# A four-stage graph network on one core: head sums in PSUM, eight edge-term slots, word rows made four sets ahead, and dense stages in two-bank instructions

## The reference

```python
# block 0, four layers, then a layer norm and two linear layers with layer norms
agg = jax.ops.segment_sum(x[src], dst, num_segments=N)
h = (1.0 + eps[i]) * x + agg
h = jax.nn.relu(_bn(h @ W1[i] + b1[i], bn1_g[i], bn1_b[i]))
h = _bn(h @ W2[i] + b2[i], bn2_g[i], bn2_b[i])
if i < L - 1:
    h = jax.nn.relu(h)
h = _bn(h, obn_g[i], obn_b[i])
...
x = h + x_in
# block 1: x @ W_S, plus a segment sum of x[col] @ W_T and edge terms
# block 2, four layers
msg = jax.nn.relu(x[src] + ea)
h = x + jax.ops.segment_sum(msg, dst, num_segments=n)
h = jax.nn.silu(h @ W1[l] + b1[l]) @ W2[l] + b2[l]
# block 3, attention with 8 heads of 16
score = K[src] * Q[dst] / jnp.sqrt(jnp.float32(dh)) * Eh
score = jnp.exp(jnp.clip(score.sum(-1, keepdims=True), -5.0, 5.0))
wV = jax.ops.segment_sum(V[src] * score, dst, num_segments=N)
Z = jax.ops.segment_sum(score, dst, num_segments=N)
h_attn = (wV / (Z + ATTN_EPS)).reshape(N, D)
```

## Time and profile before

| | us |
|---|---|
| runs | 10679.4, 10709.26, 10701.52 |
| median | 10701.52 |
| profiled execution | 10682.69 |
| span of its trace | 10681.0 |

### The profile page before, as it was taken

One profiled execution on the slowest core, in us unless ns is written; L12 is line 12 of the kernel. 1 busy time (PEld: TensorE's weight loads), 2 busy tenths in 40 slices (PEclk: granted clock), 3 DMA queues, 4 the chain that ended last, 5 costly groups with the idle time before them and its releaser, 6 DMA issues.

```text
span 10681.0 us, 246329 instructions
## 1 busy us (share of the span) xinstructions
PE 7847.9 (73%) x65479; PEld 6767.7 (63%) x65480; DVE 7303.3 (68%) x17259; ACT 3898.0 (36%) x7935; POOL 4320.5 (40%) x4160
## 2 busy tenths in 40 slices
PE   4689884667777776865489887787777777597775
PEld 3466663556676676765368676676676666586664
DVE  7476663345755755756656568878778778648998
ACT  0122121320520611602450263553553543575665
POOL 0677674556035044063005306316226136006664
PEclk7555555789899898988699999999899999799997
DMA  8666668466485584673189679689689589398885
GB/s 337 179 196 192 189 189 113 157 235 174 175 290 159 206 267 131 262 242 99 47 248 421 251 291 329 230 304 328 222 309 330 218 312 329 134 385 255 249 247 160
DMA packets 1666229, 2508.24 MB, mean 235 GB/s; under 512 B 406323, under 2 KB 930348, under 8 KB 1665680
## 3 DMA queue, kind: packets, MB, share of 16 engines
q1 hardware_dynamic: 1230926, 1418.34, 40.2%
q0 software_dynamic: 305856, 1048.98, 28.3%
q10 hardware_dynamic: 129282, 39.02, 1.6%
HBM read 1485.24 MB, written 1091.81 MB: 241 GB/s over the span
## 4 chain that ended last, share of the span: by engine, by line
PE 24%; issue 10%; DVE 10%; ACT 2%; SPq 2%; DVEq 1%; DMA 1%; ACTq 0%; POOL 0%; another core or an unknown queue 0%; POOLq 0%
PE ps L949 8%; PE ps L977 6%; PE ps L974 4%; PE ps L944 3%; SPq L691 2%; DVE heads L1800 1%; DVE gath L1812 1%; DVE gath L1795 1%; DVE gath L1733 1%; DVE weights L1781 1%; ACT gath L1262 1%; ACT gath L1220 1%; DVE big L1790 0%; ACT big L1394 0%; DVEq L541 0%
## 5 line engine op out<-in xcount | busy, mean ns | idle before, releaser
L805 POOL DMA_INDIRECT gath<-msg_units,unit_at_d x2176 | 2154.6, 990 | 3606.5 <-DMA msg_units<-gath 2387.8
L977 PE MATMUL ps<-onehot,gath 128*128 128x125 f32 x17408 | 2500.2, 299 | 980.8 <-issue 412.2
L977 PEld LDWEIGHTS ps<-onehot,gath 128*128 128x128 f32 x17408 | 2258.6, 208 | 1222.4 <-issue 936.9
L949 PE MATMUL ps<-big,onehot 125*128 x29376 | 2017.3, 227 | 395.0 <-ACT gath L1220 213.4
L949 PEld LDWEIGHTS ps<-big,onehot 125*128 125x128 bf16 x29376 | 1871.6, 99 | 541.6 <-issue 483.3
L1668 DVE TENSOR_SCALAR onehot<-row_b,part 125x512 bf16<-125x512 uint8 x2720 | 1267.8, 483 | 1076.5 <-PE ps L949 620.5
L1220 ACT ACTIVATE gath<-ps 128x512 f32<-128x512 f32 x2448 | 1417.3, 597 | 1000.4 <-PE ps L949 654.9
L1726 DVE TENSOR_TENSOR onehot<-ps,node_d 128x500 f32<-128x500 f32 x2176 | 1462.7, 673 | 185.3 <-issue 161.7
L1745 DVE TENSOR_TENSOR big<-big,ps 128x125 f32 x2176 | 609.3, 280 | 775.6 <-PE ps L977 718.4
L779 POOL DMA_INDIRECT rec<-big,idx_ring x832 | 966.1, 1161 | 417.4 <-issue 342.4
L1262 ACT ACTIVATE gath<-gath 128x512 f32<-128x512 f32 x1088 | 685.2, 630 | 1104.4 <-issue 558.6
(11 more groups left out here) (264 smaller groups left out, 10459.8 us busy)
## 6 DMA issues: line engine op xcount, KB each, us to landing
...
kv_units<-gath SPq DMA_DIRECT2D x272, 512.0 KB
...
rec<-gath SPq DMA_DIRECT2D x272, 256.0 KB
big<-rec SPq DMA_DIRECT2D x272, 256.0 KB
...
```

Source lines behind the costliest of these rows:

```text
L805: pool.indirect_dma_start(att_slot(q) if way == "attr" else gath[:, q, :], None, units, bass.IndirectOffsetOnAxis(ap=unit_at[w][:, g:g + 1 ...
L949: ins = pe.matmul(ps[:, r, c], hots_t[0:NT, r, c], upper[0:NT, ds(at_[q] + b, D)], start=b == NA * NODES_PAD, stop=b == LOW)
L977: ins = pe.matmul(ps[:, RING + r, 0:NT], unit_ring[:, q, j, :], hots[:, r, j, :], start=j == 0, stop=j == UNIT - 1)
```

## The change

1. **Dense stages.** A sweep's five banks are handled as `SPANS`: banks 0 and 1, banks 2 and 3, and bank 4. ACT's and DVE's evictions, applications, additions and `bn_stats` each take one span, so there are three instructions to a sweep instead of five, two of them over 500 columns. `bn_aggr` combines 15 partial results instead of 25. PE still works and counts by single banks; banks are freed two at a time. Loops of 25 single-block trips become 5 trips of 3 spans.
2. **Head sums.** `head_sums` writes PSUM bank 4, and `clamp` reads it there and writes `heads` in SBUF; before, it went from SBUF to SBUF.
3. **Edge-term slots.** `eh_r` has 8 slots instead of 4. SP's load of group g waits for `scores_made` of group g-8 instead of `attn_ready` of g-4. SP issues it ahead of that iteration's row load, which is now for group g itself, in a ring of 4 quarter rows, and waits for `q_hot` of g-4.
4. **Word rows of pass 0.** Casts, transposes, copies and stores run four sets ahead instead of two, and the load back three sets ahead instead of two. The four casts, transposes, copies, stores and three loads of the first sets stand before the loop, and DVE waits for the loaded row at a set's second group instead of its third.

```diff
@@ -78,6 +78,9 @@
 SWEEPS = NBLK // SLOTS_PS
+SPANS = ((0, 2), (2, 2), (4, 1))
+NSPANS = SWEEPS * len(SPANS)
+assert sum(c for _, c in SPANS) == SLOTS_PS
@@ -420,7 +423,8 @@
         kv_r = part_of_big([P, Q, PER, 2 * D], HT * NODES_PAD + BKT * SUMS_W)
-        eh_r = part_of_big([P, RING, PER, D])
+        eh_r = part_of_big([P, Q, PER, D])
+        assert at[0] <= RE * NODES_PAD
         node_f = weights[:, 0:GROUPS * UNIT]
@@ -469,9 +473,9 @@
         divided = sem("divided")
-        kv_in, eh_in = sems("kv_in", Q), sems("eh_in")
+        kv_in, eh_in = sems("kv_in", Q), sems("eh_in", Q)
         attn_hot, attn_sums = sem("attn_hot"), sem("attn_sums")
-        q_row_in = sems("q_row_in", Q)
+        q_row_in = sems("q_row_in")
         hidden_full, hidden_free = sem("hidden_full"), sem("hidden_free")
@@ -666,10 +670,10 @@
                 if n["edges"] == 0:
-                    store_row(0, 0)
-                    store_row(0, 1)
-                    load_row(0, 0)
-                    load_row(0, 1)
+                    for k in range(SETS_LAP):
+                        store_row(0, k)
+                    for k in range(SETS_LAP - 1):
+                        load_row(0, k)
                     for c in range(DROWS):
@@ -682,11 +686,10 @@
                             k = (h * Q + q) // RING
-                            if n["edges"] == 0 and q % RING == 0:
-                                if not (last and k >= 2):
-                                    store_row(i + (k + 2) // SETS_LAP, (k + 2) % SETS_LAP)
-                            if n["edges"] == 0 and q % RING == RING - 1 and not (last and k >= 2):
-                                load_row(i + (k + 2) // SETS_LAP, (k + 2) % SETS_LAP)
+                            if n["edges"] == 0 and q % RING == 0 and not last:
+                                store_row(i + 1, k)
+                            if n["edges"] == 0 and q % RING == RING - 1 and not (last and k >= 1):
+                                load_row(i + (k + 3) // SETS_LAP, (k + 3) % SETS_LAP)
                             sp.wait_ge(evicted, base + g + 1)
@@ -714,21 +717,20 @@
                 def load_row(i, q):
-                    sp.dma_start(row_b[:, q // RING, q % RING * GSLOTS:(q % RING + 1) * GSLOTS],
+                    sp.dma_start(row_b[:, 0, q % RING * GSLOTS:(q % RING + 1) * GSLOTS],
                                  node_bytes["d"][ds((i * Q + q) * GSLOTS, GSLOTS)].partition_broadcast(P))\
-                      .then_inc(q_row_in[q], 16)
+                      .then_inc(q_row_in[q % RING], 16)
...
                         g = i * Q + q
-                        if not (last and q >= Q - RING):
-                            if not (first and q < RING):
-                                sp.wait_ge(q_hot, g - RING + 1)
-                            load_row(i + (q + RING) // Q, (q + RING) % Q)
+                        if not first:
+                            sp.wait_ge(scores_made, g - Q + 1)
+                        sp.dma_start(eh_r[:, q, :, :], rec[ds(g * GSLOTS, GSLOTS), AT_EH:AT_EH + D]
+                                     .rearrange("(p j) w -> p j w", j=UNIT)).then_inc(eh_in[q], 16)
                         if not (first and q < RING):
-                            sp.wait_ge(attn_ready, g - RING + 1)
-                        sp.dma_start(eh_r[:, q % RING, :, :], rec[ds(g * GSLOTS, GSLOTS), AT_EH:AT_EH + D]
-                                     .rearrange("(p j) w -> p j w", j=UNIT)).then_inc(eh_in[q % RING], 16)
+                            sp.wait_ge(q_hot, g - RING + 1)
+                            load_row(i, q)
                 for q in range(RING):
@@ -821,8 +823,8 @@
                     pool.wait_ge(kq_made, g + 1)
-                    pool.wait_ge(eh_in[g % RING], 16 * (g // RING + 1))
-                    pool.tensor_tensor(kq(g), kq(g), eh_r[:, g % RING, :, :], ALU.mult).then_inc(scores_made, 1)
+                    pool.wait_ge(eh_in[g % Q], 16 * (g // Q + 1))
+                    pool.tensor_tensor(kq(g), kq(g), eh_r[:, g % Q, :, :], ALU.mult).then_inc(scores_made, 1)
                     if g + AHEAD < GROUPS:
@@ -933,7 +935,7 @@
                         if n["edges"] == 0 and q % RING == 0 and not last:
-                            turn_words(i * (Q // RING) + q // RING + 2, q // RING, False)
+                            turn_words(i * (Q // RING) + q // RING + SETS_LAP, q // RING, False)
                         pe.wait_ge(row_hot, base + g + 1)
@@ -1202,8 +1211,8 @@
                             k = (h * Q + q) // RING
-                            if n["edges"] == 0 and q % RING == 0 and not (last and k >= 2):
-                                keep_words(i + (k + 2) // SETS_LAP, (k + 2) % SETS_LAP, False)
+                            if n["edges"] == 0 and q % RING == 0 and not last:
+                                keep_words(i + 1, k, False)
                             act.wait_ge(rows_mm, base + i * (2 * Q) + h * Q + q + 1)
@@ -1300,9 +1309,9 @@
                 with act.Fori(0, SWEEPS) as i:
-                    for s in range(SLOTS_PS):
-                        act.wait_ge(mm_full, base + SLOTS_PS * i + s + 1)
-                        one(i * SLOTS_PS + s, s).then_inc(mm_free, 1)
+                    for s, c in SPANS:
+                        act.wait_ge(mm_full, base + SLOTS_PS * i + s + c)
+                        one(i * SLOTS_PS + s, s, c).then_inc(mm_free, c)
                 if end:
@@ -1310,30 +1319,34 @@
                 base = n["blocks"] * NBLK
-                evacuate(n, lambda j, s: act.activation(T(dst)[:, ds(j * BLK, BLK)], ps[:, s, 0:BLK], func,
-                                                        bias=feat(bias)), g is None)
+                evacuate(n, lambda j, s, c: act.activation(T(dst)[:, ds(j * BLK, c * BLK)].rearrange("p (c w) -> p c w", w=BLK),
+                                                           ps[:, s:s + c, 0:BLK], func, bias=feat(bias)), g is None)
                 if g is not None:
...
-            def apply(dst, src, func, j):
-                act.activation(T(dst)[:, ds(j * BLK, BLK)], T(src)[:, ds(j * BLK, BLK)], func,
-                               bias=shift[:, 0:1], scale=scale[:, 0:1]).then_inc(act_blk, 1)
+            def apply(dst, src, func, j, c):
+                act.activation(T(dst)[:, ds(j * BLK, c * BLK)], T(src)[:, ds(j * BLK, c * BLK)], func,
+                               bias=shift[:, 0:1], scale=scale[:, 0:1]).then_inc(act_blk, c)
             def norm_apply(n, src, dst, func, then):
-                with act.Fori(0, NBLK) as j:
-                    apply(dst, src, func, j)
+                with act.Fori(0, SWEEPS) as i:
+                    for s, c in SPANS:
+                        apply(dst, src, func, i * SLOTS_PS + s, c)
                 root(n, mv[:, 1:2])
@@ -1660,9 +1675,9 @@
                                 dve.wait_ge(rows_mm, base + g - RING + 1)
-                            if n["edges"] == 0 and q % RING == 0 and not (last and k >= 2):
-                                cast_words(i + (k + 2) // SETS_LAP, (k + 2) % SETS_LAP, False)
-                            more = q % RING == (1 if n["edges"] else 2) and not (last and k == SETS_LAP - 1)
+                            if n["edges"] == 0 and q % RING == 0 and not last:
+                                cast_words(i + 1, k, False)
+                            more = q % RING == 1 and not (last and k == SETS_LAP - 1)
                             if more:
@@ -1674,8 +1689,8 @@
                 if n["edges"] == 0:
-                    cast_words(0, 0, True)
-                    cast_words(0, 1, True)
+                    for k in range(SETS_LAP):
+                        cast_words(0, k, k < 2)
                     for c in range(DROWS):
@@ -1795,15 +1810,18 @@
+                def head_ps(q):
+                    return ps[:, 4, q * PER * HEADS:(q + 1) * PER * HEADS]
                 def head_sums(g, q):
                     dve.wait_ge(scores_made, g + 1)
-                    sch.mark(dve.tensor_reduce(heads[:, q, :], gath[:, 6 + q % 2, :].rearrange("p (h d) -> p h d", d=DH),
+                    sch.mark(dve.tensor_reduce(head_ps(q), gath[:, 6 + q % 2, :].rearrange("p (h d) -> p h d", d=DH),
                                                mybir.AxisListType.X, ALU.add))
...
                     sch.wait()
-                    dve.tensor_scalar(heads[:, q, :], heads[:, q, :], -5.0 * DH ** 0.5, 5.0 * DH ** 0.5,
+                    dve.tensor_scalar(heads[:, q, :], head_ps(q), -5.0 * DH ** 0.5, 5.0 * DH ** 0.5,
                                       ALU.max, ALU.min).then_inc(score_ready, 1)
@@ -1852,7 +1870,7 @@
-                ch.link(dve.bn_aggr(mv[:, 0:2], stats[:, 0:NBLK * 6]))
+                ch.link(dve.bn_aggr(mv[:, 0:2], stats[:, 0:NSPANS * 6]))
                 dve.tensor_scalar(mv[:, 1:2], mv[:, 1:2], EPS, None, ALU.add).then_inc(var_ready, 1)
@@ -1863,35 +1881,39 @@
                 with dve.Fori(0, SWEEPS) as i:
```

(17 more changed lines are left out.)

137 lines of the change are left out of this document (77 added, 60 removed).

## The result

| | before | after |
|---|---|---|
| median of the runs, us | 10,696.4 | 10,573.0 |
| lowest to highest | 10,679.4 to 10,709.3 | 10,568.6 to 10,588.5 |
| profiled execution's span | 10,681.0 | 10,575.2 |

The ratio is 0.9888, with a 95% interval of 0.9875 to 0.9900: 1.1% faster. Forecast were 10,473 and a range of 10,365 to 10,560; the change gave 123 us between the medians where 229 were forecast.

The account below looks back on a forecast made before the run. Pass 0 was taken as bound by a row-load loop over four groups, attention by DVE held behind POOL's product. Gains 104 + 41 + 84 = 229 us from 10,682.7 gave 10,454, plus 19 for the median: 10,473; range 10,365 to 10,560.

Parts of the forecast that it names:

- What comes late next?: Pass 0: step seeking the next limit among POOL, SP, PE and ACT; it took 5.2 us a set.
- four-group loop: Pass 0: one-hots, product, eviction, row load and landing, some 6.7 us, cover four groups and set today's pace.
- POOL's 5.0 us: Pass 0: four word gathers 1.25 us apart make 5.0 us a set, the next floor.
- seven groups: Pass 0: the same load latency covers seven groups after the change, allowing 3.8 us a set by that loop alone.
- Rival 2: Pass 0 stays near 6.2 us a set by SP's issues or PE's low clock: 10,541 us; thirteen in a hundred.
- rival 4: Pass 0 or dense stages gain nothing, through something unseen: within 0.3% of 10,702 us; three in a hundred.
- The prologue's 10 us: Pass 0: preparing four sets instead of two before the loop starts the first one-hots 10 us later.
- The two-input rule: Attention: POOL reading SBUF contends with DVE instructions having two SBUF inputs, so the clamp is freed and `times_scores` caught.
- Rival 1: Attention: POOL's product doesn't hold `times_scores`; gain 141 us instead of 41, kernel 10,373 us; twenty in a hundred.
- The 500-column estimates: Dense stages: over 500 columns one statistics instruction takes 0.68 us and one ACT instruction 0.70 us.
- Rival 3: Attention: row loads come late behind edge-term loads and stop DVE; slower, 10,785 us; three in a hundred.
- upper bound for pass 0, 36 us of gain: Pass 0: the least gain allowed, at 6.2 us a set, with SP's or DVE's 1.2 us wait unhidden.

Follow-up runs that it names:

- e10: The changed kernel, unchanged, traced on the same chip as the kernel before: 10,482.8 us, ratio 0.9898 to the kernel before.
- e11: The changed kernel with pass 0's word rows made two sets ahead as before: 10,492.4 us, ratio 0.9906 to the kernel before.
- e2: The changed kernel, but DVE begins pass 0 only when all 272 word gathers are done: 10,712.6 us.
- e18: The changed kernel with pass 0's message writes issued by ACT and times_scores reading exponentials from PSUM: 10,371.9 us, ratio 0.9789 to the kernel before.
- e9: The kernel before, unchanged, run again for its trace: 10,589.2 us.
- e17: The kernel before, unchanged, run once more for its trace: 10,604.0 us.
- e3: The changed kernel, but ACT also writes the exponentials to PSUM, where times_scores reads them: 10,451.7 us, ratio 0.9778 to the kernel before.

## Why the prediction was right and wrong

**Pass 0, forecast 104 us, measured 3.5.** The working named the wrong limit at the step "What comes late next?". It took the four-group loop as the bound of today's 6.87 us a set, and POOL's 5.0 us as the next floor, from sums of durations and from POOL's own step. Neither was the limit. The loop did hold PE for a part of the time (45.4 us of 465 for one-hots), but with seven groups a set stayed at 6.8 to 6.9 us (e10 and e11 say the same), since PE's idle time for its own issue took the place of the wait. The gathers make PE and SP issue late, which no sum of busy times shows; the sum took PE's 4.65 us of busy time a set and left out 91.3 us of its idle time for issue. Without gathers a set is 3.8 us (e2), and there PE's work is the limit. The evidence lay in the rows: DVE idle 119.4 us for its own issue, SP's load instructions of up to 0.71 us, a DMA share of 0.42 and a clock of 0.76 where pass 1 had 0.81 and 0.99. I read SP's long instructions as part of a budget with slack, instead of asking why they were absent in pass 1. Rival 2 was of the right kind, "held near 6.2 us by SP's issues", but priced at 36 us of gain and 13 in 100; it came at 6.9 us, and not by SP (e18) but with PE's issue late. Nearest to what happened was rival 4 for pass 0, "something I didn't see", with 3 in 100 and no mechanism named. The prologue's 10 us came as forecast (9.6). That POOL's pace gives 5.3 us a set on the second kind of chip (forecast 5.2) doesn't save the term: it needed 6.87 us before, which was never measured there.

**Attention, forecast 41 us, measured 30.** The mechanism was right in each step: clamp 0.19, `times_scores` caught instead (1.23, forecast 1.2), the round 3.18 (3.1 to 3.2), waits for edge terms gone. Sizes: the head sums 20 us (forecast 26; a round gained 0.086 instead of 0.11), the slots 10 us by these two traces (forecast 15), of which e9 and e17 show that they may be anything from nothing to 16. The two-input rule was the right reading of the one row that bore on it, and e3 shows its other side: 0.68 us when one input is in PSUM. Rival 1's price, 141 us, was nearly met by e3 (146 from 922 to 776), and so was its DMA bound of 2.84 us a group: the mean round is 2.86 with DMA at 0.96.

**Dense stages, forecast 84 us, measured 77.** By stage in one layer: `linear` 3.5 (forecast 4.3), `norm_linear` 3.0 (3.5), `norm_apply` 5.4 (5.5), `norm_out` 1.6 (1.8), and 0.3 in each of three `bn_aggr`, which I hadn't counted: 14.3 with it, against 15.1, so 57 in four layers; the rest of the 63 between the spans of the four layers is drift of the sums that lie between the same one-hots. The 500-column estimates held: statistics 0.68 (0.68), ACT 0.68 to 0.73 (0.70).

**Rival 3** (rows starving in attention) didn't show: DVE has no wait for rows there.

The range failed since its upper bound for pass 0, 36 us of gain, was itself argued; a bound of nothing would have put the upper end at 10,577. That the time missed the range by only 13 us says little: it holds a term that was wrong by a hundred.
